# Causal attention on one Trainium2 core: heads normalised on GpSimd, stacked in pairs and projected together

## The chip, the cores and the metric

The kernel runs on 1 core of one Trainium2 chip. The metric is the device time of one execution in microseconds, the median of several runs.

## What is computed

`x` is 4 batches of 1024 tokens of 128 features, fp32. It is layer-normalised to `xn`, and the output is `x` plus two branches of `xn`. The branch that the change touches is causal attention with 16 heads of 64:

```python
normed = x / l2 * dim ** 0.5 * gamma
qkv = (normed @ w_qkv).reshape(b, n, 3, h, d)
sim = jnp.einsum('bhid,bhjd->bhij', q, k)      # q scaled by d ** -0.5
sim = jnp.where(causal_mask, mask_value, sim)
attn = jax.nn.softmax(sim, axis=-1)
out = jnp.einsum('bhij,bhjd->bhid', attn, v)
return out.reshape(b, n, h * d) @ w_out
```

The other branch is a mixture of 8 experts (two chosen per token, 128 to 512 to 128), added to `xn` and layer-normalised.

## The kernel before

It has four stages: `routing` (normalisation, the transposed normed tokens `nT` with an fp32r high and low part, the router, the slots for each expert), `attention([0], True, xn)` for the first pair of heads with fp32 probabilities ("native"), `experts`, and `attention([1..7], False, None)` for the other seven pairs with split probabilities. Each engine walks the same hand-written order (`beside`, L799) and takes from it what is its own; all waits are on semaphores.

**Units and chunks.** The work of attention is cut in units, one head of one batch: 8 in the first call, 56 in the second (G = 8 units per pair of heads, `g // 2` the batch, `g % 2` the head of the pair). A unit has 12 chunks of score work. For a chunk, PE multiplies keys and queries into one of two `score_ps` banks (L1298, L1299), ACT takes the exponent into `probs` and, in the second call, once more into `p_hi` (L1082, L1084), POOL masks a diagonal block (L1024) and subtracts `p_lo` (L1032), and four chunks later (LAG) PE multiplies with the values into `head_ps` (L1318 to L1327). Row 64 of the values is one, so row 64 of `head_ps` holds the sums, the softmax's denominators.

**Maxima.** Beside unit g, PE computes the scores of unit g + 1 a first time, tile by tile (8 tiles at the chunks of `MAX_AT`, L770, L1281), DVE takes their negated maxima (L1140), and SP moves each as a row into `q_b` (`shifts`, L927), where it enters the real scores as one more contraction row. A first tile's pass waits until DVE has taken the last of the unit before.

**Projections.** Even units hold the four q and k projections of the next batch (chunks 0, 1, 3, 5; `PROJECT_AT`, L773), odd units the two value projections (chunks 1 and 5; L1262, fp32, from `nT`). ACT takes high parts (L1057, L1061, L1066), DVE low parts (L1114, L1126), and SP copies q and k high parts to the second operands by DMA, 4 of 256 KB after the fourth projection (`copies`, L936, L937), all in SBUF.

**Output.** ACT copies `head_ps` (65 rows, values and sums) to `heads` (L1095). In the unit after, at chunks 7, 9 and 11 (`Y_AT`, L789), PE multiplies it with `wo` (65 rows, 129 columns: the weights of one head and a one in the corner, so that column 128 is the sum) in tiles of 128 tokens (L1341), DVE inverts column 128 (L1191) and adds rows times inverse to `acc` (L1199).

**Combine steps.** In the second call, groups of six units bring the experts' results in: POOL gathers rows (L1008) in the second and third unit, DVE centres rows of `x` in the third (L1156, chunks 2, 4, 5, 6), and the other steps lie in units 3, 5 and 7 from the group's start.

```python
            PROJECT_AT = [{0: 0, 1: 1, 3: 2, 5: 3}, {1: 4, 5: 5}]
...
            COMBINE_AT = [(2, c) for c in (2, 4, 5, 6)]
...
            Y_AT = [7, 9, 11]
            y_units = [(0, 3), (3, 3), (6, 2)]
```

## Time and profile before

| | us |
|---|---|
| median of 3 runs | 1457.95 (1456.97 to 1460.27) |
| the profiled execution | 1463.13 |
| its span, first to last instruction | 1461.4 |
| PE busy | 1351.4 (92%) |
| DVE busy | 1038.1 (71%) |
| ACT busy | 947.8 (65%) |
| POOL busy | 867.2 (59%) |
| first attention call, on PE | 66 to 242 |
| second attention call, on PE | 394 to 1457 |

Busy is the time in which an engine works on instructions; issuing DMAs, waiting and branching do not count. The profile also gives PE's granted clock as a share of 2.4 GHz, 0.958 over the whole span. In a timeline a row is one instruction or a few alike, with its start, its duration and, in brackets, the idle time ahead of it and what ended it. In a group, the number after the bar is the idle time ahead of its instructions. SPq is SP's DMA queue; its duration is that of the issue, not of the transfer.

### The profile page before, as it was taken

How to read it: one execution, taken by the hardware profiler on the slowest of the kernel's cores; microseconds unless marked ns; L12 is line 12 of the kernel's file. 1: busy time of each engine (PE TensorE's matmuls, PEld its weight loads, DVE VectorE, ACT ScalarE, POOL GpSimd, SP SyncE). 2: the span in 40 equal slices, each digit the busy share in tenths (PEclk: the TensorE clock that was granted, in tenths of full speed). 3: DMA queues.
4: the chain of work that ended last, by engine and by line, in shares of the span. 5: the costliest groups of instructions: out<-in, count | busy, mean ns of one | idle time of the engine just before them, and what ended most of it. 6: DMA issues, size and time to landing. Idle time of an engine off the chain costs nothing.

```text
span 1461.4 us, 27770 instructions
## 1 busy us (share of the span) xinstructions
PE 1351.4 (92%) x8360; PEld 1124.9 (77%) x8361; DVE 1038.1 (71%) x2674; ACT 947.8 (65%) x2094; POOL 867.2 (59%) x1304
## 2 busy tenths in 40 slices
PE   4569998999879999999999899899899999899998
PEld 4446666999757888788788788788788788788886
DVE  5656654222257788888888888888888888888773
ACT  2435544555447677677777677677677777677775
POOL 3426651332227568667667667767766766766666
PEclk9669999999869999999999999999999999999999
DMA  6222221222122022112112212112212212211112
GB/s 204 89 60 63 63 54 55 77 75 77 47 57 52 3 41 50 29 30 51 35 33 44 43 30 46 38 36 42 41 30 46 42 32 39 48 30 32 30 30 59
DMA packets 131078, 72.47 MB, mean 50 GB/s; under 512 B 80216, under 2 KB 116864, under 8 KB 130944
## 3 DMA queue, kind: packets, MB, share of 16 engines
q1 hardware_dynamic: 114304, 54.18, 18.2%
q0 software_dynamic: 4096, 8.40, 1.9%
q10 hardware_dynamic: 12544, 8.29, 1.9%
q8 instruction: 62, 1.02, 0.3%
q14 instruction: 72, 0.59, 0.1%
HBM read 20.47 MB, written 16.52 MB: 25 GB/s over the span
## 4 chain that ended last, share of the span: by engine, by line
PE 53%; DVE 11%; issue 5%; ACT 2%; DMA 1%; SPq 0%; DVEq 0%; POOLq 0%; ACTq 0%
PE max_ps L1281 8%; PE score_ps L1299 6%; PE score_ps L1298 6%; PE misc_ps L1341 6%; PE head_ps L1318 5%; PE head_ps L1327 5%; PE head_ps L1325 5%; PE head_ps L1323 5%; DVE max_ps L1140 4%; PE misc_ps L1262 3%; DVE x_row L1156 2%; PE misc_ps L1256 2%; DVE q_a L1126 1%; PE misc_ps L1257 1%; PE misc_ps L1258 1%
## 5 line engine op out<-in xcount | busy, mean ns | idle before, releaser
L1032 POOL TENSOR_TENSOR p_lo<-probs,p_hi 128x512 fp32r<-128x512 f32 (+3 forms) x560 | 536.1, 958 | 188.5 <-ACT p_hi L1084 183.9
L1082 ACT ACTIVATE probs<-score_ps 128x512 f32<-128x512 f32 (+3 forms) x768 | 377.5, 492 | 257.0 <-PE score_ps L1299 243.8
L1140 DVE CUSTOM_DVE_ANT_0 max_ps<-max_ps,mask 128x128 f32<-128x128 f32 (+7 forms) x512 | 390.7, 763 | 111.1 <-PE max_ps L1281 87.8
L1298 PE MATMUL score_ps<-q_a,k_a 128*128 128x512 f32 (+3 forms) x768 | 304.3, 396 | 0.2 <-ACT p_hi L1084 0.2
L1281 PE MATMUL max_ps<-k_a,q_a 128*128 128x512 f32 (+3 forms) x768 | 238.6, 366 | 54.2 <-DVE shift L1140 45.0
L1024 POOL TENSOR_SCALAR_AFFINE_SELECT probs<-probs 128x128 f32<-128x128 f32 x512 | 153.7, 300 | 202.3 <-ACT p_hi L1084 136.9
L1299 PE MATMUL score_ps<-q_b,k_b 65*128 65x512 f32 (+3 forms) x768 | 269.6, 351 | 0.0
L1084 ACT ACTIVATE p_hi<-score_ps 128x512 fp32r<-128x512 f32 (+3 forms) x560 | 263.1, 470 | 0.0
L1318 PE MATMUL head_ps<-probs,v_all 128*65 128x128 f32 (+3 forms) x1088 | 248.7, 310 | 0.0
L1281 PEld LDWEIGHTS max_ps<-k_a,q_a 128*128 128x128 f32 x768 | 140.8, 195 | 114.9 <-DVE shift L1140 86.5
L1323 PE MATMUL head_ps<-p_hi,v_hi 128*65 128x512 f32 (+3 forms) x560 | 210.3, 376 | 0.0
L1327 PE MATMUL head_ps<-p_lo,v_hi 128*65 128x512 f32 (+3 forms) x560 | 183.8, 328 | 0.0
L1325 PE MATMUL head_ps<-p_hi,v_lo 128*64 128x512 f32 (+3 forms) x560 | 183.3, 327 | 0.0
L1298 PEld LDWEIGHTS score_ps<-q_a,k_a 128*128 128x128 f32 x768 | 146.9, 191 | 45.7 <-issue 15.7
L1299 PEld LDWEIGHTS score_ps<-q_b,k_b 65*128 65x128 f32 x768 | 147.5, 192 | 23.7 <-issue 10.8
L1199 DVE SCALAR_TENSOR_TENSOR acc<-misc_ps,rden,acc 128x128 f32<-128x128 f32 x512 | 150.2, 346 | 6.8
L1318 PEld LDWEIGHTS head_ps<-probs,v_all 128*65 128x65 f32 x1088 | 136.8, 138 | 21.7 <-issue 1.5
L1341 PE MATMUL misc_ps<-wo,heads 65*128 65x129 f32 x1024 | 149.1, 280 | 2.6 <-ACT heads L1095 1.5
L1341 PEld LDWEIGHTS misc_ps<-wo,heads 65*128 65x128 f32 x1024 | 142.9, 196 | 9.6 <-issue 2.9
L1095 ACT ACTIVATE heads<-head_ps 65x512 f32<-65x512 f32 x128 | 76.1, 595 | 43.4 <-PE head_ps L1327 26.4
L530 POOL CAST w_now<-w1T 128x1024 fp32r x39 | 40.6, 1042 | 106.0 <-PE hidden L664 87.8
L1126 DVE TENSOR_TENSOR q_a<-misc_ps,q_a 64x512 fp32r<-64x512 f32 x128 | 88.3, 690 | 20.9 <-ACT q_a L1057 17.0
(165 smaller groups left out, 2086.6 us busy)
## 6 DMA issues: line engine op xcount, KB each, us to landing
k_a<-k_a SPq DMA_DIRECT2D x64, 256.0 KB
q_b<-q_a SPq DMA_DIRECT2D x64, 256.0 KB
q_b<-shift SPq DMA_DIRECT2D x512, 0.5 KB
sorted_x<-zeros SPq DMA_DIRECT2D x13, 384.0 KB, 5.0
rows<-sorted_x SPq DMA_DIRECT2D x39, 128.0 KB, 2.1
sorted_y<-result ACTq DMA_DIRECT2D x39, 128.0 KB, 1.8
acc<-in_L_attn_x_dram SPq DMA_DIRECT2D x4, 512.0 KB, 7.2
x_row<-in_L_attn_x_dram SPq DMA_DIRECT2D x8, 256.0 KB
```

The lines of the kernel that those rows point to most:

```text
L1032: pool.tensor_tensor(p_lo[:, lo_slot(g, c), w0:w1], probs[:, slot, w0:w1], p_hi[:, slot, w0:w1].bitcast(F32), ALU.subtract).then_inc(pool_ ...
L1082: ins = act.activation(probs[:, slot, 0:width], src[:, 0:width], ACT.Exp, scale=SCALE)
L1084: ins = act.activation(p_hi[:, slot, FROM[c]:width], src[:, FROM[c]:width], ACT.Exp, scale=SCALE)
L1140: dve.tensor_tensor_reduce(out=max_ps[:, at:at + width], in0=max_ps[:, at:at + width], in1=mask[:, SEQ - width:SEQ], scale=-1.0, scalar=-M ...
L1281: ins = pe.matmul(max_ps[:, at + k0:at + k1], q_a[i][s][:, t * P:(t + 1) * P], k_a[i][s][:, k0:k1], start=True, stop=True)
L1298: pe.matmul(dst, k_a[i][s][:, keys], q_a[i][s][:, qs], start=True, stop=False)
L1299: pe.matmul(dst, k_b[i][s][:, keys], q_b[i][s][:, qs], start=False, stop=True).then_inc(scores_ready, 1)
L1318: ins = pe.matmul(head_ps[0:HEAD + 1, q0:q0 + end], v_all[i][:, j, s], probs[:, slot, 0:end], start=(j == 0), stop=(c in LAST and not SPLI ...
L1323: pe.matmul(head_ps[0:HEAD + 1, cols], v_hi[i][:, j, s], p_hi[:, slot, w0:width], start=(j == 0 and not DIAG[c]), stop=False)
L1325: pe.matmul(head_ps[0:HEAD, cols], v_lo[i][:, j, s], p_hi[:, slot, w0:width], start=False, stop=False)
L1327: ins = pe.matmul(head_ps[0:HEAD + 1, cols], v_hi[i][:, j, s], p_lo[:, lo_slot(g, c), w0:width], start=False, stop=c in LAST)
L1341: ins = pe.matmul(dst[:, t * (D + 1):(t + 1) * (D + 1)], heads[:, g % 2, q0:q0 + P], wo[:, g % 2], start=True, stop=True)
```

## The change

**Heads of a pair together.** `heads` becomes `raw`, with the same ACT copy. For each unit W but the last two of each call (`stacks`):
- in unit W + 1, chunk 5, SP moves the sums, row 64 of `raw`, by DMA to `sums`, 128 partitions of 8; at chunk 8 DVE inverts them (`invert`); at chunk 10 SP writes them to `inverse_row` in DRAM;
- in unit W + 2, chunk 0, SP reads that row back into `rden_all`, once for each of 64 partitions; after chunks 3 and 4 POOL multiplies `raw` by it, 64x512 each, into rows 0 to 63 or 64 to 127 of `stacked` (`normalise`), and waits for each of the two to end;
- in the odd unit W + 2 of a pair's second head, at chunks 7 and 9, PE multiplies `stacked` (128 rows) with `wo` (both heads' weights, 128 columns), four tiles each, and DVE adds each bank to `acc` in one addition of 128x512 (`add_y`).

The last pair of each call goes the old way (`last_y`, with `wo_last`).

**Values' tokens.** `nT` is kept no longer. `routing` stores it in DRAM (`nT_dram`, 8 DMAs of SP), and ACT's queue loads 512 KB per batch into `tokens` in the even unit ahead of the value projections. The freed space holds `probs` and `rden_all`, so the first exponents and the first spread wait for the stores.

**Order.** One order runs over all pairs of a call. The q and k projections come half by half (q and k of tokens 0 to 511, then the others), and the copies are 4 of 128 KB after the second projection and 4 after the fourth. At the start of a call only tiles 0 to 3 of the first unit's maxima stand ahead of the first score; the other four come in its chunks 0 and 1, and the next unit's maxima at chunks 2 to 10. The last batch's output is stored in three pieces. Additions of `acc` by combine steps and by `add_y` wait for each other.

```diff
+            HALF_TILES = TILES // 2
+            FIRST_MAX_AT = [0, 0, 1, 1]
+            SECOND_MAX_AT = [2, 3, 4, 5, 6, 7, 8, 10]
-            Y_AT = [7, 9, 11]
+            Y_AT = {7: 0, 9: 1}
+            LAST_Y_AT = {8: 0, 10: 1, 11: 2}
+            def stacks(W):
+                return W0 <= W < WL - 2
+                    if W % 2 and c in Y_AT and stacks(W - 2):
+                        order += [(kind, W // 2 - 1, Y_AT[c]) for kind in ("y", "add")]
+                    if stacks(W - 1):
+                        order += [(kind, W - 1, 0) for kind, at in (("sums", 5), ("invert", 8), ("inverse", 10))
+                                  if at == c]
+                    if stacks(W - 2):
+                        order += [(kind, W - 2, n) for kind, n, at in (("spread", 0, 0), ("norm", 0, 3),
+                                                                      ("norm", 1, 4)) if at == c]
...
+                        if kind == "project" and c in (1, 3):
+                            copies(g, c // 2)
+                        if kind == "shift":
+                            shifts(g, c)
+                        if kind == "sums":
+                            W = g
+                            sp.wait_ge(heads_out[0], W + 2)
+                            sp.wait_ge(heads_out[1], W + 2)
+                            sp.dma_start(sums[:, W % 2], raw[HEAD:HEAD + 1, W % 2]).then_inc(sums_moved[W % 2], 16)
+                        if kind == "inverse":
+                            sp.wait_ge(sums_inverted, n_stacked(W) + 1)
+                            sp.dma_start(inverse_row[W % 2].rearrange("(p j) -> p j", p=P), inverse[:, W % 2]
+                                         ).then_inc(inverse_moved[W % 2], 16)
+                        if kind == "spread":
+                            sp.wait_ge(inverse_moved[W % 2], n_spread(W) * 16)
...
+                                sp.wait_ge(norm_done, 2 * n_stacked(W - 1) + 2)
+                            sp.dma_start(rden_all[:], inverse_row[W % 2].partition_broadcast(HEAD)
+                                         ).then_inc(spread[W % 2], 16)
...
+                    def normalise(W, half):
+                        s, cols = W % 2, slice(half * BANK, (half + 1) * BANK)
+                        rows = slice(s * HEAD, (s + 1) * HEAD)
+                        if half == 0:
+                            pool.wait_ge(spread[s], n_spread(W) * 16)
...
+                        pool.tensor_tensor(stacked[rows, cols], raw[0:HEAD, s, cols], rden_all[:, cols],
+                                          ALU.mult).then_inc(norm_done, 1)
+                        pool.wait_ge(norm_done, 2 * n_stacked(W) + half + 1)
...
+                    def load_tokens(Q):
...
+                        act.dma_start(tokens[:], nT_dram[:, cols]).then_inc(tokens_loaded, 16)
...
+                    def invert(W):
+                        dve.wait_ge(sums_moved[W % 2], n_spread(W) * 16)
+                        if W - W0 >= 2:
+                            dve.wait_ge(inverse_moved[W % 2], n_spread(W - 2) * 16)
+                        dve.reciprocal(inverse[:, W % 2], sums[:, W % 2]).then_inc(sums_inverted, 1)
+                    def add_y(Q, n):
...
+                        dve.tensor_tensor(rows, misc_ps[u % 2][:].rearrange("p (t d) -> p t d", d=D), rows,
+                                          ALU.add).then_inc(y_added, 1)
...
+                    def project_pair(Q, n):
...
+                            ins = pe.matmul(dst[:, q * D:(q + 1) * D], stacked[:, q0:q0 + P], wo[:],
+                                            start=True, stop=True)
```

**DVE, from the end of chunk 5 of an even unit.** Before: the last of the projections' low parts is ahead, `ISA max_ps,shift` are the maxima of tiles 5 to 7, and an additions' block follows each.

```order
L1140 ISA max_ps,shift<-max_ps,mask 128x768 [waits max_scores,max_taken]
L1140 ISA shift 128x1
L1191 RECIPROCAL rden<-misc_ps_2 128x3 [waits misc_ready]
L1199 SCALAR_TENSOR_TENSOR acc<-misc_ps_2,rden,acc 128x128 [waits recip_done]
L1199 SCALAR_TENSOR_TENSOR acc<-misc_ps_2,rden,acc 128x128 x2
```

Now:

```order
L1186 ISA max_ps,shift<-max_ps,mask 128x768 [waits max_scores,max_taken]
L1186 ISA shift 128x1
L1186 ISA max_ps,shift<-max_ps,mask 128x896 [waits max_scores,max_taken]
L1186 ISA shift 128x1
L1237 RECIPROCAL inverse<-sums 128x8 [waits inverse_moved1,sums_moved1]
L1186 ISA max_ps,shift<-max_ps,mask 128x1024 [waits max_scores,max_taken]
L1186 ISA shift 128x1
L1186 ISA max_ps,shift<-max_ps,mask 128x128 [waits max_scores,max_taken]
```

The additions are gone from the even unit, and the wait for the sums' DMA stands ahead of the last maximum.

**SP, the same two units.** `q_b_2<-shift` are the shifts, `k_a_2<-k_a_2` and `q_b_2<-q_a_2` the copies. Before:

```order
L936 DMA k_a_2<-k_a_2 64x1024 [waits hi_done]
L937 DMA q_b_2<-q_a_2 64x1024
L936 DMA k_a_2<-k_a_2 64x1024
L937 DMA q_b_2<-q_a_2 64x1024
L927 DMA q_b_2<-shift 1x128x1 [waits max_taken] x16
```

Now, from the second copies of an even unit to the spread of the next:

```order
L931 DMA k_a_2<-k_a_2 64x512 [waits hi_done]
L932 DMA q_b_2<-q_a_2 64x512
L931 DMA k_a_2<-k_a_2 64x512
L932 DMA q_b_2<-q_a_2 64x512
L923 DMA q_b_2<-shift 1x128x1 [waits max_taken]
L949 DMA sums<-raw 128x1x8 [waits heads_out1,heads_out0]
L923 DMA q_b_2<-shift 1x128x1 [waits max_taken] x2
L953 DMA inverse_row<-inverse 128x8 [waits sums_inverted]
L923 DMA q_b_2<-shift 1x128x1 [waits max_taken]
L963 DMA rden_all<-inverse_row 64x1024 [waits norm_done,inverse_moved1]
```

The sums' DMA stands behind the copies and a shift.

**POOL, chunks 2 to 5 of a unit without gathers.** Before, with the masks (`AFFINE_SELECT`) and the splits (`p_lo`):

```order
L1032 TENSOR_TENSOR p_lo<-probs,p_hi 128x256 [waits pv_done]
L1024 AFFINE_SELECT probs<-probs 128x128 [waits probs_ready]
L1032 TENSOR_TENSOR p_lo<-probs,p_hi 128x128 [waits pv_done]
L1032 TENSOR_TENSOR p_lo<-probs,p_hi 128x512 [waits pv_done,probs_ready]
L1024 AFFINE_SELECT probs<-probs 128x128 [waits probs_ready]
```

Now:

```order
L1070 TENSOR_TENSOR p_lo<-probs,p_hi 128x256 [waits pv_done]
L1061 AFFINE_SELECT probs<-probs 128x128 [waits probs_ready]
L1070 TENSOR_TENSOR p_lo<-probs,p_hi 128x128 [waits pv_done]
L1033 TENSOR_TENSOR stacked<-raw,rden_all 64x512 [waits pool_split,diag_masked,misc_ready,spread0]
L1070 TENSOR_TENSOR p_lo<-probs,p_hi 128x512 [waits pv_done,probs_ready,norm_done]
L1033 TENSOR_TENSOR stacked<-raw,rden_all 64x512 [waits diag_masked,pool_split]
L1061 AFFINE_SELECT probs<-probs 128x128 [waits norm_done,probs_ready]
```

A multiply stands behind each of the splits of chunks 3 and 4.

## Rows read from the trace of the kernel before

**Rows 1.** Busy time by stretch: us, busy per engine (x instructions), clock, DMA share
```profile
420.00:1449.00 1029.00, 994.26 (x6190) 829.84 (x6189) 842.59 (x2144) 755.33 (x1670) 707.49 (x1069) 0.98 0.20 38
...
1361.00:1398.00 37.00, 37.00 (x239) 31.58 (x238) 26.58 (x68) 29.14 (x65) 24.52 (x38) 1.00 0.18 30
...
1243.00:1261.00 18.00, 15.81 (x87) 12.72 (x86) 17.21 (x32) 11.67 (x26) 14.86 (x22) 0.91 0.38 78
```

**Rows 2.** Waits of PE, 420 to 1449 us: us in total, times, longest
```profile
PE max_ps L1281 <- DVE shift L1140: 33.5, 44, 2.2
```

**Rows 3.** Timeline of PE, one output projection: start us, us, engine, line
```profile
901.69 0.83 PE L1341 MATMUL misc_ps<-wo,heads 65*128 65x129 f32 x6
902.36 0.38 PE L1318 MATMUL head_ps<-probs,v_all 128*65 128x128 f32 x2
```

**Rows 4.** Timeline of PE, the maxima's first pass, in two successive units
```profile
1387.67 0.22 PE L1281 MATMUL max_ps<-k_a,q_a 128*128 128x128 f32 x1
...
1405.56 0.23 PE L1281 MATMUL max_ps<-k_a,q_a 128*128 128x128 f32 x1
```

**Rows 5.** Timeline of PE, the same pass, and a wait, around a unit that centres rows
```profile
906.04 0.23 PE L1281 MATMUL max_ps<-k_a,q_a 128*128 128x128 f32 x1
...
920.75 0.81 PE L1281 MATMUL max_ps<-k_a,q_a 128*128 128x512 f32 x2 [2.15 <-DVE shift L1140]
...
928.23 0.22 PE L1281 MATMUL max_ps<-k_a,q_a 128*128 128x128 f32 x1
```

**Rows 6.** Groups by line and shape: xcount, busy us, mean ns, idle before
```profile
L1032 POOL TENSOR_TENSOR p_lo<-probs,p_hi 128x512 fp32r<-128x512 f32 x224 | 288.4, 1287 | 185.9 <-ACT p_hi L1084 183.9 <-PE head_ps L1327 1.4
...
L1199 DVE SCALAR_TENSOR_TENSOR acc<-misc_ps,rden,acc 128x128 f32<-128x128 f32 x512 | 150.2, 346 | 6.8
...
L1114 DVE TENSOR_TENSOR v_lo<-misc_ps,v_hi 128x512 fp32r<-128x512 f32 x56 | 38.7, 692 | 67.7 <-ACT v_hi L1066 67.7
```

**Rows 7.** Timeline of POOL, chunks 3, 4 and 6 of an even unit
```profile
1210.94 0.47 POOL L1032 TENSOR_TENSOR p_lo<-probs,p_hi 128x128 fp32r<-128x128 f32 x1
...
1213.45 1.29 POOL L1032 TENSOR_TENSOR p_lo<-probs,p_hi 128x512 fp32r<-128x512 f32 x1 [2.04 <-ACT p_hi L1084]
...
1216.34 1.28 POOL L1032 TENSOR_TENSOR p_lo<-probs,p_hi 128x512 fp32r<-128x512 f32 x1 [1.35 <-ACT p_hi L1084]
```

**Rows 8.** Timeline of ACT, SP and DVE, chunks 5 to 10 of the unit of rows 4
```profile
1396.54 1.21 ACT L1057 ACTIVATE k_a<-misc_ps 64x512 fp32r<-64x512 f32 x2
...
1399.61 1.21 SPq L937 DMA_DIRECT2D q_b<-q_a  x1
...
1400.56 1.10 DVE L1140 CUSTOM_DVE_ANT_0 max_ps<-max_ps,mask 128x896 f32<-128x896 f32 x1
...
1403.44 1.23 DVE L1140 CUSTOM_DVE_ANT_0 max_ps<-max_ps,mask 128x1024 f32<-128x1024 f32 x1 [0.26 <-PE max_ps L1281]
```

**Rows 9.** DMA issues: xcount, KB each, median us from issue to landing
```profile
sorted_x<-zeros SPq DMA_DIRECT2D x13, 384.0 KB, 5.0
rows<-sorted_x SPq DMA_DIRECT2D x39, 128.0 KB, 2.1
```

**Rows 10.** Timeline of PE and DVE at the starts of both attention calls
```profile
80.95 0.79 PE L1281 MATMUL max_ps<-k_a,q_a 128*128 128x128 f32 x2 [3.74 <-DMA q_b<-q_a]
...
83.50 0.70 DVE L1140 CUSTOM_DVE_ANT_0 max_ps<-max_ps,mask 128x512 f32<-128x512 f32 x1
...
92.25 0.63 PE L1298 MATMUL score_ps<-q_a,k_a 128*128 128x512 f32 x1
...
408.66 0.79 PE L1281 MATMUL max_ps<-k_a,q_a 128*128 128x128 f32 x2 [3.79 <-DMA q_b<-q_a]
```

**Rows 11.** Timeline of DVE and POOL, unit of rows 5
```profile
914.92 1.78 DVE L1156 TENSOR_SCALAR x_row<-x_row,mean,rstd 128x128 f32<-128x128 f32 x1
...
915.31 1.30 POOL L1032 TENSOR_TENSOR p_lo<-probs,p_hi 128x512 fp32r<-128x512 f32 x1
```

**Rows 12.** Timeline of SP: the last store
```profile
1457.79 0.37 SPq L968 DMA_DIRECT2D out_dram<-acc  x1
```

More of the change, by code:

```diff
@@ L89, in attention_and_experts @@
         zeroed = sem("zeroed")
+        nT_stored = [sem(f"nT_stored{i}") for i in range(BATCH)]
+        tokens_loaded = sem("tokens_loaded")
         dve_step = sem("dve_step")
@@ new lines, in attention @@
+            order = ([(kind, Q0, n) for n in range(6) for kind in ("project", "project_lo")]
+                     + [("max", W0, t) for t in range(HALF_TILES)] + [("shift", W0, t) for t in range(HALF_TILES)])
+            for at in range(W0 * CH, WL * CH + LAG):
+                order += beside(at // CH, at % CH)
+            order += [(kind, WL - 1, n) for n in range(len(y_units)) for kind in ("last_y", "last_add")]
+            misc = [o for o in order if o[0] in ("project", "y", "last_y")]
@@ L1360, in _ @@
-                    run(walk, pe)
+                    for kind, g, c in order:
+                        if kind == "score":
+                            score(g, c)
+                        elif kind == "max":
+                            max_scores_of(g, c)
+                        elif kind == "project":
+                            project(g, c)
+                        elif kind == "pv":
+                            values(g, c)
+                        elif kind == "y":
+                            project_pair(g, c)
+                        elif kind == "last_y":
+                            project_last(g, c)
```

643 lines of the change are left out of this document (330 added, 313 removed).

## The prediction

> **What bounds the kernel now.** I read the busy time by stretch first. From 420 to 1449 us, nearly all of the second attention call with its 56 units, PE is busy for 994.26 of 1029 us at a granted clock of 0.98, and in a stretch without combine steps for 37.00 of 37.00 us, while DVE, ACT and POOL have 26.58, 29.14 and 24.52 us [rows 1]. So there each microsecond taken from PE comes off the time until another engine is in the way, and ACT (79%) is the next one. Second, PE's waits: in that call it waits for hardly anything but DVE's maxima, 33.5 us in 44 waits [rows 2]. Third, the lengths of units: an undisturbed even unit takes 1405.56 - 1387.67 = 17.89 us [rows 4]; one in which DVE also centres rows takes 928.23 - 906.04 = 22.19 us, though PE waits only 2.15 us in it [rows 5]. The other 2 us or so go with PE at 1.2 in place of 2.4 GHz for a while after such a wait: the granted clock is 0.91 in a stretch around another such unit, where it is 1.00 in the stretch without [rows 1]. A wait of 2 us therefore costs 4.3 us. That price matters below.
>
> **Term A, the output projection.** Six PE records of one projection go by in 902.36 - 901.69 = 0.67 us, 0.112 us each [rows 3] (the modelled durations overlap; the step is what counts). Before, 64 units issue 16 records each, 1024. Now 30 pairs issue 16 each, and the last pair of each call, 4 units, still 16 each: 544. 480 records fewer, of 0.112 us: **-53.8 us**, 48.4 of it in the second call. The 128 rows in place of 65 lengthen no stream, since the step follows the columns (128 for 129). All of it lies on the path by rows 1, since PE has no idle time there to swallow it. It comes out of even units alone: they lose all 16 records, odd ones keep their number.
>
> **Term B, the starts of the calls.** PE now waits 3.74 and 3.79 us for the last copy before the first maximum [rows 10]. The copies of the first half now start two projections earlier and land while PE still projects the values, so these waits go. The first score comes 92.25 - 80.95 = 11.3 us after the first maximum [rows 10]; now it needs only tiles 0 to 3, taken by 83.50 + 0.70 = 84.2, and their shifts' landing, some 2.1 us like the shortest in rows 9: 86.3, up to 5.9 us earlier. But the four maxima put off run in unit 0 on a DVE that has 12 of them there, so I let most of that be given back. 5 us per call, **-10 us**; bounds 0 and -2 x (3.75 + 5.9) = -19.
>
> **Term C, the end.** The last store is 512 KB, issued at 1457.79 [rows 12] in a span of 1461.4: 3.6 us. Its last piece is now 128 KB, which takes 2.1 us from issue to landing [rows 9]. **-1 us**.
>
> **Term D, DVE's relief.** A unit's 8 additions of about 0.29 us (150.2 us over 512) [rows 6] and three reciprocals become, per pair, two additions of 128x512 from PSUM, like the 692 ns of v_lo [rows 6], and two small reciprocals. DVE loses some 2 us per unit. Of the 33.5 us of waits, 6 x 2.15 lie in the units with centring, ahead of the place where the additions stood; about 17 us are small waits of 0.2 to 1.2 us in other units, and half of them should go: **-8 us** (0 to -20).
>
> **Term E, the new wait on DVE.** This is the term that I trust least. `invert` stands in DVE's order at chunk 8, ahead of the last maximum, and waits for the denominators' DMA. SP issues that DMA at chunk 5, in even units behind the four copies of the second half and one shift. In the unit of rows 4, ACT ends the last key copy at 1396.54 + 1.21 = 1397.75, and the fourth 256 KB copy has been issued at 1399.61 + 1.21 = 1400.8 [rows 8]; with copies of half the size the fourth may be through in half that time, 1400.2. The shift's issue adds about the 0.37 us of another short issue [rows 12], and landing at least 2.1 us [rows 9]: 1402.7 to 1403.3, and up to 0.6 us later if the sums queue behind what the copies still move. `invert` takes 0.2, and the maximum of 1024 columns, which can start only then, 1.23 [rows 8]: it ends at 1404.1 to 1405.3, with its read of 0.1 at 1404.2 to 1405.5. PE needs it at the next unit's first maximum, which now comes 1.78 us earlier, at 1405.56 - 1.78 = 1403.8 [rows 4]. PE waits 0.4 to 1.7 us; I take 0.9, in 27 even units of the second call: **+24 us** (11 to 46). In odd units SP has no copies ahead of the sums, and the same chain ends before chunk 8. The rest of the relay (inverse sums to DRAM at chunk 10, spread at chunk 0, 256 KB) has until chunk 3's multiply; it fits with about 1 us over, and POOL's gap there takes as much again.
>
> No row shows in what order two DMAs of one queue move. The Trainium skill, DMA: Bandwidth & Descriptors, "Two DMAs through the same engine are not ordered", says that the descriptors of one queue of one DMA engine start in order; by that the sums' would start behind the copies', at the late end of this range, and the whole sum would be 22 us higher (46 for 24).
>
> **Term F, POOL.** 120 multiplies of 64x512 are new. No row shows one; between 128x128 at 0.47 us [rows 7] and 128x512 at 1287 ns [rows 6] I take 1.29, since a lane does its 512 columns. 2.6 us per unit, on an engine with 24.52 us of 37 [rows 1]. They stand behind the splits of chunks 3 and 4: in the unit shown POOL is idle 2.04 us ahead of chunk 4's split and 1.35 us ahead of chunk 6's [rows 7], and PE reads a split only four chunks after its score. So they are **free** there. Without that cover they would cost up to 2.6 us a unit. In the 16 units with gathers the gaps are filled; I add **+3 us** (0 to 20).
>
> **Term G, ACT.** 29.14 us of 37 over an even and an odd unit [rows 1] leave room, but an even unit shrinks to about 16.1 us with ACT's projection copies and one token DMA more in it, and PE has only two score banks. 0.1 us per even unit: **+3 us** (0 to 14). The token loads (512 KB per pair of units) and the store of nT lie beside other work: DMA is busy 20% [rows 1].
>
> **Sum**: -53.8 - 10 - 1 - 8 + 24 + 3 + 3 = -42.8. The profiled execution took 1463.1 us (span 1461.4), so 1420.3 for it. The median of the runs is 1457.95, 5.2 below; the forecast for the runs is **1415 us**. Its own range, from the bounds that can go together, is 1400 to 1435.
>
> **The rivals.**
> 1. *The sums land in time* (chance 0.27). If small DMAs overtake the tail of the copies or land in under 1.5 us, Term E is gone: 1391. For it: no row shows so small a DMA, and 2.1 us is what 128 KB take. Against it: the fourth copy's issue ends 3 us after ACT's last key copy [rows 8], however soon the sums land.
> 2. *Slower: DVE waits over 2 us in every even unit* (0.10). The same place, another price. At the 5.0 us that rows 9 show for 384 KB, the sums land at about 1406, PE waits 3 us, and like the unit of rows 5 the clock falls after it; at the 4.3 us of such a unit or more, 27 x 4.3 = 116 in place of 24: 1507. It decides from 24 + 43 = 67 us, 2.5 us per even unit, so from a wait of some 2 us with its loss of clock. Against it: 4 KB are not 384.
> 3. *The multiplies hold DVE* (0.10). In the units with centring, a DVE operation of 128x128 between SBUF tiles takes 1.78 us while POOL's 1.30 us split runs beside it, and ends as that ends [rows 11]. If three of the four centrings of each of the 8 units meet one multiply more, 3 x 1.29 x 8 = 31: 1446. For it: POOL is without gaps there. Against: POOL waits for its own multiply, which leaves a gap for DVE. The Trainium skill, GPSIMD Engine Reference, "Key points", says that GpSimd shares its SBUF interfaces with VectorE, with contention for DVE instructions in a two-port mode or with two SBUF inputs; the row agrees with it.
> 4. *POOL is late* (0.05): the spread lands after POOL has reached the multiply, and PE waits for splits, 1 us in half the units: 1443.
>
> **How the numbers follow.** The forecast has 0.48. 1380 to 1455 holds it, rivals 1, 3 and 4 with their spread, and leaves out rival 2 and the far ends, together under 0.2. A measurement of this kernel tells 0.2%, 2.9 us, from no change. Slower is rival 2 and a tail of 3 and 4: 0.12. Within 0.2%: 0.03. Faster: 0.85. That the change does not do what it says has one place only, the last pair of each call, and it is in Term A.
>
> **What would show it.** Right: 544 records of the projection; PE's busy time in the second call 45 to 50 us lower; even units some 16.8 to 17 us, odd ones near 17; a DVE wait of `inverse` for the sums' DMA, in even units alone, followed by a PE wait at the next unit's first maximum. Rival 1: no such wait, even units near 16.2. Rival 2: those waits near 3 us and the clock below 0.95 in the second call. Rival 3: centring operations over 2 us. Rival 4: POOL's `stacked` waiting for the spread. Wrong altogether: PE's busy time unchanged, or ACT as the one that PE waits for.

## The result: 1559.5 us, slower by 100 us, and the profile after

The changed kernel takes 1559.53 us (median of 4 runs, 1557.23 to 1563.08) where the kernel before took 1459.11 on the same chip: a ratio of 1.069, 95% interval 1.066 to 1.072. The forecast was 1415. The profiled execution of the change took 1560.88 us.

The page of the change: busy time, the clock row and the DMA line.

```profile
PE 1365.7 (88%) x7880; PEld 1108.6 (71%) x7881; DVE 944.4 (61%) x2134; ACT 940.2 (60%) x2094; POOL 1015.3 (65%) x1424
...
PEclk9679999999688998999999999899899999899999
...
DMA packets 169509, 107.67 MB, mean 69 GB/s; under 512 B 101240, under 2 KB 138144, under 8 KB 169376
```

PE issues 7880 matmul records where it issued 8360: the 480 records are gone. But its clock row falls to 8 in the second call, where before it stands at 9, and POOL has 1015 us where it had 867. The busy time by stretch of the second call (columns as in [rows 1]), and its waits:

```profile
420.00:1549.00 1129.00, 1013.31 (x5767) 817.49 (x5765) 762.51 (x1662) 748.02 (x1670) 840.42 (x1177) 0.94 0.26 60
```

```profile
PE max_ps L1345 <- DVE shift L1186: 100.4, 75, 3.3
DVE inverse L1237 <- DMA sums<-raw: 72.5, 26, 3.4
...
DVE x_row L1206 <- DMA two_y<-sorted_y,slots: 29.4, 8, 4.0
...
ACT raw L1143 <- POOL stacked L1033: 22.0, 10, 3.2
...
PE score_ps L1362 <- DMA q_b<-shift: 5.0, 1, 5.0
```

The stretch takes 1129 us where the 1029 us of [rows 1] did the same work. PE waits 100.4 us for maxima in place of 33.5 [rows 2]. Two waits on DVE are new: for the sums (72.5 us) and for the gathered rows (29.4 us in 8 waits of up to 4.0). One on ACT is new as well: its copy of `head_ps` into `raw` waits for the POOL multiply that still reads that buffer (22.0 us in 10). One place at a time.

**The end of an even unit.** Timeline of SP's queue, from the copies of the second half on:

```profile
1494.85 0.50 SPq L931 DMA_DIRECT2D k_a<-k_a  x1
...
1496.68 0.60 SPq L932 DMA_DIRECT2D q_b<-q_a  x1
1497.32 0.62 SPq L923 DMA_DIRECT2D q_b<-shift  x1
1498.04 0.57 SPq L949 DMA_DIRECT2D sums<-raw  x1
```

DVE, in the same stretch:

```profile
1501.86 0.20 DVE L1237 RECIPROCAL inverse<-sums 128x8 f32<-128x8 f32 x1 [3.07 <-DMA sums<-raw]
1502.05 1.23 DVE L1186 CUSTOM_DVE_ANT_0 max_ps<-max_ps,mask 128x1024 f32<-128x1024 f32 x1
```

PE, in the same stretch:

```profile
1503.49 0.30 PE L1345 MATMUL max_ps<-k_a,q_a 128*128 128x128 f32 x1 [1.79 <-DVE shift L1186]
```

Four copies and a shift are issued ahead of the sums, which go out at 1498.04 and release the reciprocal 3.8 us later. The maximum of 1024 columns stands behind it, and PE waits 1.79 us. Two units earlier the same wait also costs clock. Timeline of PE, the first pass of the maxima at three successive units:

```profile
1447.39 0.23 PE L1345 MATMUL max_ps<-k_a,q_a 128*128 128x128 f32 x1
...
1466.00 0.30 PE L1345 MATMUL max_ps<-k_a,q_a 128*128 128x128 f32 x1 [1.68 <-DVE shift L1186]
...
1484.74 0.22 PE L1345 MATMUL max_ps<-k_a,q_a 128*128 128x128 f32 x1
```

Busy time in the stretch behind the wait (the third last number is the clock):

```profile
1466.00:1470.50 4.50, 4.50 (x24) 4.17 (x25) 1.54 (x5) 1.46 (x4) 1.33 (x3) 0.68 0.28 59
```

The even unit takes 18.61 us where [rows 4] show 17.89. The odd one behind it takes 18.74 us without a further wait, because PE runs at a mean of 0.68 of 2.4 GHz for 4.5 us, so partly at 1.2 GHz. PE waits like this at the start of 20 of the odd units, mostly for 1.7 to 2.0 us.

**Unit 3 of each group of six**, the one with the first steps behind the centring. Timeline of POOL, the second multiply of the unit ahead and the last gather:

```profile
845.10 1.25 POOL L1033 TENSOR_TENSOR stacked<-raw,rden_all 64x512 f32<-64x512 f32 x1
...
853.81 0.97 POOL L1044 DMA_INDIRECT two_y<-sorted_y,slots  x1 [0.16 <-issue]
```

DVE, the first combine steps:

```profile
857.02 2.88 DVE L1206 SCALAR_TENSOR_TENSOR x_row<-two_y,weights,x_row 128x128 f32<-128x128 f32 x2 [3.65 <-DMA two_y<-sorted_y,slots]
```

PE, and below it the busy time of the unit:

```profile
860.36 0.80 PE L1345 MATMUL max_ps<-k_a,q_a 128*128 128x512 f32 x1 [3.27 <-DVE shift L1186]
```

```profile
852.60:877.80 25.20, 20.69 (x115) 16.59 (x114) 16.48 (x34) 12.63 (x30) 17.27 (x26) 0.86 0.10 22
```

The unit begins at 852.6; POOL issues the last gather 1.2 us into it. In the kernel before that came at 925.59, 2.6 us ahead of the unit that starts at 928.23 [rows 5]. DVE waits 3.65 us for it ahead of a maximum, PE 3.27 us, and the clock is 0.86 over a unit of 25.2 us. Before, the unit took 18.9.

The lengths of all units, from first pass to first pass, show where the 100 us lie. Means over seven groups, in us, units 0 to 5 of a group: 18.2, 17.6, 21.4, 19.1, 17.9 and 17.4 before; 18.9, 20.3, 20.6, 25.2, 19.0 and 18.8 in the change. Units 1 and 3 lose most, unit 2 even gains.

**The start of the second call**, in PE's timeline:

```profile
415.32 0.76 PE L1362 MATMUL score_ps<-q_a,k_a 128*128 128x512 f32 x1 [3.09 <-DMA q_b<-shift]
...
434.16 0.77 PE L1362 MATMUL score_ps<-q_a,k_a 128*128 128x512 f32 x1 [5.03 <-DMA q_b<-shift]
```

The waits of [rows 10] for the copies are gone, but the score of chunk 4 waits 5.03 us for the shifts of the unit's own tiles.

### The profile page after: what moved, and what is told of

The parts are those of the page before. It is cut to its first block, busy times and chain, and to the rows that moved or that the text cites. A ratio compares the mean times of both kernels' runs of the same rounds, so it can differ in the third digit from the quotient of the medians.

```text
span 1559.2 us, 27266 instructions
## 1 busy us (share of the span) xinstructions
PE 1365.7 (88%) x7880; PEld 1108.6 (71%) x7881; DVE 944.4 (61%) x2134; ACT 940.2 (60%) x2094; POOL 1015.3 (65%) x1424
## 3 DMA queue, kind: packets, MB, share of 16 engines
q1 hardware_dynamic: 148128, 72.65, 19.8%
## 4 chain that ended last, share of the span: by engine, by line
PE 37%; DVE 12%; issue 8%; DMA 6%; POOL 4%; SPq 4%; ACT 3%; DVEq 0%; POOLq 0%; ACTq 0%
PE max_ps L1345 6%; DMA sums<-raw 4%; DVE max_ps L1186 4%; PE score_ps L1363 4%; PE score_ps L1362 4%; PE head_ps L1392 4%; PE head_ps L1390 4%; PE head_ps L1388 3%; PE misc_ps L1326 3%; PE head_ps L1383 3%; PE misc_ps L1403 2%; DVE x_row L1206 2%; POOL p_lo L1070 2%; PE misc_ps L1318 2%; DMA two_y<-sorted_y,slots 2%
## 5 line engine op out<-in xcount | busy, mean ns | idle before, releaser
L1345 PE MATMUL max_ps<-k_a,q_a 128*128 128x512 f32 (+3 forms) x768 | 247.8, 379 | 114.3 <-DVE shift L1186 113.8
L1362 PE MATMUL score_ps<-q_a,k_a 128*128 128x512 f32 (+3 forms) x768 | 314.1, 409 | 20.9 <-DMA q_b<-shift 15.8
L1363 PE MATMUL score_ps<-q_b,k_b 65*128 65x512 f32 (+3 forms) x768 | 275.3, 358 | 0.0
L1383 PE MATMUL head_ps<-probs,v_all 128*65 128x128 f32 (+3 forms) x1088 | 256.8, 319 | 0.5 <-POOL probs L1061 0.5
L1388 PE MATMUL head_ps<-p_hi,v_hi 128*65 128x512 f32 (+3 forms) x560 | 217.6, 389 | 1.7 <-POOL p_lo L1070 1.6
L1383 PEld LDWEIGHTS head_ps<-probs,v_all 128*65 128x65 f32 x1088 | 144.4, 143 | 33.3 <-issue 1.9
L1033 POOL TENSOR_TENSOR stacked<-raw,rden_all 64x512 f32<-64x512 f32 x120 | 153.5, 1279 | 15.8 <-POOL p_lo L1070 6.5
L1143 ACT ACTIVATE raw<-head_ps 65x512 f32<-65x512 f32 x128 | 76.2, 596 | 102.3 <-PE head_ps L1392 66.8
L1172 DVE TENSOR_TENSOR q_a<-misc_ps,q_a 64x512 fp32r<-64x512 f32 x128 | 88.2, 689 | 36.9 <-ACT q_a L1094 34.2
L1172 DVE TENSOR_TENSOR k_b<-misc_ps,k_a 64x512 fp32r<-64x512 f32 x128 | 87.8, 686 | 19.8 <-ACT k_a L1094 18.8
L1392 PEld LDWEIGHTS head_ps<-p_lo,v_hi 128*65 128x65 f32 x560 | 78.9, 141 | 28.3 <-issue 3.0
```

The source lines that it names most:

```text
L1172: ins = dve.tensor_tensor(lo, src[s * HEAD:(s + 1) * HEAD, :], hi, ALU.subtract)
L1345: ins = pe.matmul(max_ps[:, at + k0:at + k1], q_a[i][s][:, t * P:(t + 1) * P], k_a[i][s][:, k0:k1], start=True, stop=True)
L1362: pe.matmul(dst, k_a[i][s][:, keys], q_a[i][s][:, qs], start=True, stop=False)
L1363: pe.matmul(dst, k_b[i][s][:, keys], q_b[i][s][:, qs], start=False, stop=True).then_inc(scores_ready, 1)
L1383: ins = pe.matmul(head_ps[0:HEAD + 1, q0:q0 + end], v_all[i][:, j, s], probs[:, slot, 0:end], start=(j == 0), stop=(c in LAST and not SPLI ...
L1388: pe.matmul(head_ps[0:HEAD + 1, cols], v_hi[i][:, j, s], p_hi[:, slot, w0:width], start=(j == 0 and not DIAG[c]), stop=False)
```

## The experiments

The theory at the outset: three places where something small stands behind something large in an engine's order. The rival: POOL's multiplies hold the units themselves. All kernels of this part ran beside the kernel before, and each time is a median. Some build on others; each says on which. Units of a group are counted from its start, unit 0: the "third" (unit 3) holds the first steps behind the centring, the "second" (unit 2) the last gathers and the centring, and the "first" (unit 1) the last 13 steps of the group before.

**The sums, three ways**, on the change as it was.

```diff
-  (("sums", 5), ("invert", 8), ("inverse", 10))
+  (("sums", 5), ("invert", 10), ("inverse", 10))   # first
+  (("sums", 4), ("invert", 8), ("inverse", 10))    # second
+  (("sums", 4), ("invert", 10), ("inverse", 10))   # third
```

> The edit: DVE inverts the sums at chunk 10, behind the unit's last maximum, in place of chunk 8, ahead of it; nothing else moves. Theory A (the reciprocal that waits for the sums' DMA holds back the last maximum, and PE with it, and the clock falls after that wait): PE's waits at the next unit's first maximum go from 1.8 to under 0.5 us in the 27 even units of the second call, and 1.5 us of half-speed clock go with each: 27 x 3.3 = 89 us less than the change's 1560, so about 1470. Theory B (POOL, with 2.6 us of multiplies more per unit, is what holds the even units): the reciprocal's place is of no matter, the time stays within 10 us of 1560. Theory C (the stall moves: the wait for the inversion now stands in SP's order ahead of the last shift and the spread, which come later): the DVE wait goes, another takes half of it back, about 1515.

> The edit: SP issues the sums' DMA at chunk 4, ahead of the four copies of chunk 5, in place of behind them; the inversion stays at chunk 8. Theory A (the sums come late because they stand behind the copies on SP's queue): DVE's wait for the sums in even units goes (28 waits, 80 us before), the landing is 2 us as in odd units in place of 3.8, and the time is about 1470 as with the late inversion. Theory B (POOL): within 10 us of 1560. Theory D (the landing of 4 KB is late for another reason, the spread or the tokens' load on the same engines): the wait stays at over 2 us and the time within 20 us of 1560.

> Both edits: the sums' DMA at chunk 4, the inversion at chunk 10. Theory A: the two take away one and the same wait, so the time is within 10 us of the better of the two single ones, about 1465. If they add up (say 1510 each alone and 1465 together), each hides a part of its own. Theory B: about 1560.

Measured: 1501.3, 1497.0 and 1498.6 us (ratios to the kernel before 1.028, 1.025, 1.026, each with 0.003 either way). Each of the two edits alone takes off some 60 us, both together no more: one wait, as Theory A had it, though 60 us and not 89. Theory A counted 3.3 us for each of 27 even units with the odd one behind it. By the means of the second kernel, units 0 and 1 together get 3.0 us shorter and units 4 and 5 together 3.4, but units 2 and 3 only 0.4: there unit 3 waits for the gathered rows all the same, and keeps its 25.2 us. Theory B falls for the units without that second stall. Of Theory C something is left: in the first kernel POOL waits for the spread, 14.1 us in 8 waits in the second call. The same place in the second kernel, on SP's queue:

```profile
1426.97 0.54 SPq L949 DMA_DIRECT2D sums<-raw  x1
1428.01 0.51 SPq L931 DMA_DIRECT2D k_a<-k_a  x1
```

DVE in the same unit:

```profile
1431.81 0.20 DVE L1237 RECIPROCAL inverse<-sums 128x8 f32<-128x8 f32 x1
```

PE, the first pass of the maxima around the odd unit ahead of it:

```profile
1400.87 0.23 PE L1345 MATMUL max_ps<-k_a,q_a 128*128 128x128 f32 x1
...
1417.90 0.22 PE L1345 MATMUL max_ps<-k_a,q_a 128*128 128x128 f32 x1
```

The sums go out ahead of the copies, and the reciprocal waits for nothing. The odd unit takes 17.03 us, where it took 18.74.

**The sums on ACT's queue.** Base: the change. The DMA is ACT's in place of SP's, at chunk 5, then at 6, then at 7.

```diff
-  sp.dma_start(sums[:, W % 2], raw[HEAD:HEAD + 1, W % 2])
+  act.dma_start(sums[:, W % 2], raw[HEAD:HEAD + 1, W % 2])
```

> The change as it was, but the sums' DMA is issued on ACT's queue at chunk 5, behind ACT's copies of the fourth projection, in place of SP's queue at the same chunk behind the four copies of k and q; the inversion stays at chunk 8. Theory Q (what makes the sums late in even units is their place on SP's queue: four issues of 0.6 us and a shift ahead of them, and 512 KB of copies on the same queue): DVE's waits for the sums, 80 us in 28, fall under 20 us, and the time is within 15 us of the kernel with the DMA at chunk 4, about 1500. Rival (the DMA engines are busy with the copies, whichever queue the sums are on): the waits stay over 50 us and the time over 1535.

> As the kernel with the sums on ACT's queue (1497 us), but one chunk later, at chunk 6, so that they are issued while SP issues the copies. Order of one queue: on a queue of their own the sums land 1.9 to 2.2 us after their issue in even units too, DVE waits for them little or not, time 1495 to 1505. Load of the DMA engines: they land 3 us or more after their issue, as on SP's queue behind the copies, DVE waits for them in most even units, 10 us in all or more.

> As the last kernel, with the sums' DMA at chunk 7 of ACT's order, so that it is issued about 1.5 us after the first copy, ahead of the tokens' load on its own queue. Order of one queue: it lands 2 us or so after its issue, the reciprocal waits under 0.5 us or not at all, time about 1497. Load of the DMA engines: it lands 3 us or more after its issue, DVE waits 1 us or more for it in even units (20 us or more in all), time 1505 or more.

Measured: 1496.9, 1496.6 and 1499.0 us; DVE waits for the sums in no unit of the three. In the first two ACT's queue issued them 1.2 and 0.5 us ahead of SP's first copy, so these tell the place only. In the third they go out in the middle of the copies. ACT's queue:

```profile
1435.43 0.48 ACTq L1135 DMA_DIRECT2D sums<-raw  x1
```

SP's queue, the first and the last copy:

```profile
1434.76 0.50 SPq L931 DMA_DIRECT2D k_a<-k_a  x1
...
1436.58 0.60 SPq L932 DMA_DIRECT2D q_b<-q_a  x1
```

DVE:

```profile
1438.55 0.20 DVE L1236 RECIPROCAL inverse<-sums 128x8 f32<-128x8 f32 x1
```

The trace has the landing of these issues: this one lands 2.4 us after it went out, where on SP's queue behind the copies it was 3.8 us to the reciprocal. Over the 27 even units of the second call the median is 2.4 us, over the odd ones, without copies, 1.9. So beside copies in flight on another queue the sums lose 0.5 us, behind them on the same queue some 1.8. That speaks for the order of the queue and against the load of the DMA engines, with two limits: here only two copies had been issued ahead of the sums, not four, and in six second units, beside POOL's gathers, they took 2.8 to 4.9 us on ACT's queue as well.

**The first combine steps three chunks later**, on top of both edits of the sums:

```diff
-  COMBINE_AT += [(g, c) for g in (3, 5) for c in (0, 0, 1, 2, 3, 4, 5, 5, 6, 7, 8, 9, 11, 11)]
+  COMBINE_AT += [(3, c) for c in (3, 3, 4, 4, 5, 5, 6, 7, 8, 9, 10, 10, 11, 11)]
+  COMBINE_AT += [(5, c) for c in (0, 0, 1, 2, 3, 4, 5, 5, 6, 7, 8, 9, 11, 11)]
```

> Both edits as before, and in the third unit of each group of six the combine steps that read the gathered rows begin at chunk 3 in place of chunk 0 (the last two of the fourteen end at chunk 11 as before). Theory A2 (a second stall: POOL's multiplies make the gathers 3 us late, DVE waits 3.7 us for them ahead of a maximum, PE waits 3.3 us and the clock falls): those 9 units go from 25.2 us to about 19, so 8 x 6 = 48 us less than the kernel with both edits, about 1420. Theory B2 (POOL is short of time in these units whatever DVE does): PE then waits for the splits in place, and not more than 15 us come back.

Measured: 1459.4 us, ratio 0.9998 (0.9983 to 1.0012), so 39 us less. The third units go from 25.2 us and more to between 19.8 and 21.0, by Theory A2. These two repairs bring the kernel to the time of the one before, and no lower.

**The own shifts ahead of the copies**, on top of that:

```diff
   order += [("max", *item) for item in max_items(W, c)]
+  order += [("shift", *item) for item in max_items(W, c) if item[0] == W]
...
-  order += [("shift", *item) for item in max_items(W, c - 1)]
+  order += [("shift", *item) for item in max_items(W, c - 1) if item[0] > W]
```

> On top of the same kernel: in the first unit of each call SP issues the shifts of that unit's own tiles 4 to 7 right behind their maxima, ahead of the four copies of the next batch's first half, in place of behind them. Theory S (the start's gain is given back because those shifts stand behind the copies on SP's queue, and the score of chunk 4 waits 5.05 us for them in the second call): that wait falls under 2 us, 3 to 5 us less per call, 6 to 10 in all, about 1451. Rival (the maxima themselves are late, DVE at 2.17 us waits there): the wait keeps its place, under 2 us of gain.

Measured: 1442.4 us, ratio 0.989 (0.987 to 0.991), 17 us less where 6 to 10 were expected; the profiled executions differ by 11 (1453.5 and 1442.8). SP's queue at the start of the second call, without the edit (copies, then the shifts):

```profile
419.04 0.50 SPq L932 DMA_DIRECT2D k_a<-k_a  x1
...
421.53 2.54 SPq L924 DMA_DIRECT2D q_b<-shift  x4
```

With it:

```profile
409.57 3.26 SPq L925 DMA_DIRECT2D q_b<-shift  x2
413.37 0.50 SPq L933 DMA_DIRECT2D k_a<-k_a  x1
```

The last own shifts now stand ahead of the copies, and the wait of 5 us for them is gone.

**The multiplies on DVE**, at chunks 4 and 5, on top of the kernel with the late first steps, then with the own shifts too, then on the change as it was:

```diff
-  if o[0] == "norm": normalise(o[1], o[2])       # in POOL's walk
+  elif kind == "norm": normalise(g, c)           # in DVE's walk, dve.tensor_tensor
-  ("norm", 0, 3), ("norm", 1, 4)
+  ("norm", 0, 4), ("norm", 1, 5)
```

> On top of the last kernel (sums' DMA at chunk 4, inversion at chunk 10, first combine steps at chunk 3): DVE does the multiplies into stacked, at chunks 4 and 5, in place of POOL at 3 and 4. Theory L (POOL's longer work stretches the combine steps: DVE operations of 128x128 between SBUF tiles take 0.8 to 1.2 us while POOL works on its tiles, 172 us of DVE in all in place of 137 before the change): those rows go back to about 137 us or below, the units with combine steps get 2 us shorter on average over 16 to 24 of them, time about 1425. Rival (DVE becomes the bound: 120 multiplies of some 0.7 us or, if they are stretched beside POOL's splits, 1.3 us are added to an engine that has 17 of 19.2 us in the first unit of each group): those units grow by 1.4 to 2.6 us each, time 1475 or more.

> Both of the two edits above. If they are independent, their gains add: about 1417 by theories L and S. If DVE is the bound at the start as well, the sum falls short by what the multiplies put ahead of the maxima of the first units.

> The change as it was, with nothing moved but the multiplies into stacked, which DVE does at chunks 4 and 5. Theory A2 (POOL's multiplies are what delays the gathers by 3 us, so that DVE waits for them in the third unit of each group): DVE's 8 waits for two_y, 29 us in the change, fall under 5 us in all and those units go from 25.2 to about 20; the waits for the sums in even units stay (80 us or somewhat less). Time about 1560 - 40 = 1520. Rival (the gathers are late because their data lands late, behind the 35 MB of new transfers): the waits for two_y stay near 29 us, the time near 1560.

Measured: 1546.0, 1531.3 and 1538.9 us. Theory L's remedy fails and its rival holds: 87 and 89 us slower than the same kernels with POOL. The group of the multiplies on DVE, in the first of the three:

```profile
L1245 DVE TENSOR_TENSOR stacked<-raw,rden_all 64x512 f32<-64x512 f32 x120 | 136.9, 1145 | 12.1 <-DMA rden_all<-inverse_row 10.4
```

137 us of DVE, 1145 ns each, where one that begins while POOL is idle takes 0.69 us (the row at 1423.69 of that trace). They stand ahead of maxima, and PE's waits for these are 115.8 us in the second call, in place of 48.3. In the third of the three, the waits for the gathered rows fall from 29.4 to 3.7 us, as Theory A2 had it, yet only 21 us come off. So the price of the multiplies was still open. The second of the three is 15 us faster than the first: the own shifts give the same again.

**The multiplies left out.** `stacked` holds ones; the relay and all waits stay. On top of the kernel of 1442 us, and on the change as it was:

```diff
-  pool.tensor_tensor(stacked[rows, cols], raw[0:HEAD, s, cols], rden_all[:, cols], ALU.mult).then_inc(norm_done, 1)
+  pool.sem_inc(norm_done, 1)
```

> On top of the kernel of 1442 us (sums at 4, inversion at 10, first steps at 3, own shifts first): POOL's 120 multiplies into stacked are left out (stacked holds ones; the relay of sums, inversion, spread and all waits stay). It prices the multiplies. Theory L (POOL's 2.6 us more per unit holds the units with gathers and stretches the combine steps): the three long units of each group (19.3, 20.0 and 20.6 us) fall together by 4 us or more, 8 x 4 = 32 us or more, so 1410 or less; units without combine steps stay at 16.8 and 17.05. Rival (those units are bound by DVE's own work and by gathers, as before the change, where they took 17.6, 22.2 and 18.9): less than 10 us come off, over 1432.

> The change as it was, with POOL's 120 multiplies left out (stacked holds ones; every wait stays). Theory M (the multiplies make the gathers late): DVE's waits for two_y, 29 us in 8, go to under 3 us, the third unit of each group from 25.2 to about 19.5; the waits for the sums stay, since they come from SP's queue. Time: 1559 - 8 x 5.5 (third units) - 36 (what the multiplies cost the repaired kernel, less some 10 us that are the same thing) = about 1490. Rival (the gathers are late for the DMA traffic): the third units keep 24 us or more, the time over 1530.

Measured: 1406.4 us (36 less) and 1507.4 us (52 less). Busy time of units 1, 2 and 3 of a group, in the kernel of 1442 us:

```profile
1091.30:1110.50 19.20, 17.68 (x115) 14.39 (x114) 16.99 (x35) 12.49 (x30) 15.31 (x22) 1.00 0.18 43
1110.50:1130.30 19.80, 17.35 (x95) 13.11 (x94) 14.97 (x30) 15.00 (x33) 17.25 (x23) 1.00 0.45 112
1130.30:1151.00 20.70, 17.98 (x116) 14.48 (x115) 16.77 (x33) 12.27 (x29) 18.38 (x26) 1.00 0.11 21
```

And without the multiplies:

```profile
1176.40:1193.90 17.50, 17.06 (x115) 14.51 (x114) 13.74 (x34) 12.02 (x29) 12.39 (x20) 1.00 0.15 35
1193.90:1211.60 17.70, 16.70 (x96) 13.21 (x94) 13.52 (x29) 14.73 (x33) 15.18 (x21) 1.00 0.56 129
1211.60:1230.50 18.90, 17.67 (x116) 14.54 (x114) 15.36 (x33) 12.45 (x30) 15.21 (x24) 1.00 0.14 30
```

In the first unit of the group, 1.7 us go; DVE, which does the same operations, is busy 3.3 us less in it. The 36 us are a low price: in two of the eight groups the second unit takes 23.8 and 23.4 us without the multiplies, where most others take 17.7; PE waits 3.0 us there for a maximum behind centrings, and its clock is 0.86. These 12 us are a new stall; without it, by this estimate, 48 would have come off. In the change as it was, the waits for gathered rows fall from 29.4 to 10.9 us, not to under 3, and the third units go from 25.2 to between 19.4 and 22.5 us, 4.6 on average, some 36 of the 52 us. Most of the rest is in the first units, 20.3 to 18.4 us on average. Theory M is right in kind and short in size; what else makes the gathers late, no run isolates. The waits for the sums stay (84.3 us).

**Where the steps stand.** On the kernel of 1442 us, gathers earlier; steps spread; both; and the kernel before with the same spread:

```diff
-  GATHER_AT = [(1, 8)] + [(1, c) for c in (9, 10, 11)] + [(2, c) for c in (1, 3, 5, 7, 9)]
+  GATHER_AT = [(1, 8)] + [(1, c) for c in (9, 10, 11)] + [(2, c) for c in (0, 1, 2, 5, 7)]
...
+  COMBINE_AT += [(3, c) for c in (3, 4, 5, 6, 7, 8, 9, 10, 11)]      # in place of the steps behind the centring
+  COMBINE_AT += [(4, c) for c in (7, 7, 8, 9, 9, 11)]
+  COMBINE_AT += [(5, c) for c in range(12)]
+  COMBINE_AT += [(6, c) for c in (7, 7, 9, 9, 10, 11)]
+  COMBINE_AT += [(7, c) for c in range(8)]
```

> On top of the same kernel of 1442 us: POOL issues the second unit's five gathers at chunks 0, 1, 2, 5 and 7 in place of 1, 3, 5, 7 and 9. Theory: POOL is behind from chunk 5 on in these units, because its multiplies stand there too; with two gathers less behind them, the last splits come earlier, 0.5 to 1 us less in each of 8 units, about 1437. Rival (POOL has the same work in all, and its early part delays the splits that PE waits for): 1442 or up to 8 us more.

> On top of the same kernel of 1442 us: the 41 combine steps behind the centring are spread over five units (9, 6, 12, 6 and 8) in place of three (14, 14, 13). DVE no longer has eight additions in even units, where it is now busy 12 of 16.8 us. Theory: the first unit of each group, which holds the last 13 steps and takes 19.25 us with DVE busy for 17, gets 1 to 2 us shorter, the third the same, and the two even units that take steps stay within 0.3 us: 8 x 2.5 = 20 us less, about 1422. Rival (each step is stretched wherever POOL works beside it, and the even units give it back): 1435 to 1450.

> The kernel of 1424.7 us with the second unit's gathers at chunks 0, 1, 2, 5 and 7. Alone this gave 2 us, within its uncertainty. Expected: 1420 to 1426. If the third unit, whose steps now begin thinner, no longer gains from it, 1425 or above.

> The kernel before, with nothing but the table of the combine steps as in the kernel of 1424.7 us (9, 6, 12, 6 and 8 steps in five units, the first behind chunk 3). Theory P (in the kernel before, even units hold eight additions with scaling on DVE, so they have no room for six steps more; and its gathers were in time): the time stays within 6 us of 1459, and the whole 34 us of the repaired kernel are owed to the pairing. Rival (the spread helps any kernel, since odd units lose two to five steps): 1445 or less, and the pairing is worth only the rest.

Measured: gathers early 1440.5 us, 2 less, inside the uncertainty. Spread: 1424.7 us, ratio 0.976 (0.974 to 0.979), 17.7 less, as expected. Both: 1427.4, nothing gained. The kernel before with the spread: 1441.2 us, ratio 0.989 (0.986 to 0.991). That went against Theory P: the spread helps the kernel before by 18 us as well. So of the 34 us between the best version, 1424.7, and the kernel before, 18 are the spread's, and the pairing with its three repairs is worth 16.5.

## Why the prediction was wrong, step by step

**What bounds the kernel** was right as to PE, and that it waits for DVE's maxima: in the best version still 27.8 us. ACT, named as the next engine in the way by its busy share, was not that: PE waits 5.0 us for it in the second call of the change, and 100.4 for the maxima.

**Term A** holds in its count (480 records) and its reach. Without stalls an odd unit takes 17.03 us, as forecast, and an even one 16.8. That this is also the 16.8 to 17 us of the forecast is luck: those were 16.1 with a wait of 0.9 on top. An even unit loses 1.1 us against [rows 4], not 1.79. The remaining 0.7 us are steps between matmuls beyond the shortest of their shapes: summed over an even unit, 2.5 us in the kernel of 1442 us, 1.7 in the one before. One, of 0.33 us, carries a wait for ACT's exponent; the others have no releaser in the trace. So **Term G** (0.1 us) was mis-sized at this place by 0.7, some 19 us over 27 units, as far as they are ACT's.

**Term B** (-10) failed on its second half. The waits for copies went, as said. But I looked for what gives the gain back on DVE, and it was on SP: the copies of the next batch stand ahead of the shifts of the unit's own second half. From the first projection to the start of its second unit, the second call took 439.49 - 393.58 = 45.9 us before and 448.95 - 397.90 = 51.1 in the change, so +5 in place of -5; with the shifts ahead it is 43.5. The first call, up to its third unit, took 65.2 and 65.5 us.

**Term C** (-1) is too small to be told apart: the last three stores are issued from 1555.12 on, and the span ends at 1559.2. **Term D** (-8) did not show: DVE's busy time in the second call fell from 842.6 to 762.5 us, but PE's waits for maxima are 43.4 us even in the kernel of 1442 us, against 33.5 [rows 2]. With the multiplies left out of that kernel they are 26.8: the relief was there, and the longer combine steps (below) took it.

**Term E** (+24, bounds 11 to 46) had the right place, the right order of events and the wrong price: 60 us. From the end of ACT's last key copy, 1494.82, to the reciprocal it is 7.0 us, where I had 5.0 to 6.2. The sums go out 3.2 us after that copy, and land 3.8 us later, not 2.1 to 2.7. PE's wait, mostly 1.7 to 2.0 us, lay at the edge of my range; that it also lowers the clock I had kept for waits of over 2 us, in rival 2. This is the step that failed in the term: it priced the wait alone, and the wait with its loss of clock costs some 3.2 us where nothing else holds the pair of units, nothing much where the rows are late too, and 60 / 27 = 2.2 us on average. The Trainium skill, DMA: Bandwidth & Descriptors, "Two DMAs through the same engine are not ordered", has descriptors of one queue start in order; the 3.8 us behind copies, and 2.4 us on another queue beside them, agree with it, and the price by it (46) was the nearer one.

**Term F** (+3, bounds 0 to 20) is the step that failed most. One multiply takes what I had estimated:

```profile
L1033 POOL TENSOR_TENSOR stacked<-raw,rden_all 64x512 f32<-64x512 f32 x120 | 153.5, 1279 | 15.8 <-POOL p_lo L1070 6.5 <-POOL probs L1061 1.0
```

But they are not free. Left out, they give back 52 us in the change and 36 in the repaired kernel. I had read POOL's gaps in a unit without combine steps [rows 7], and there the multiplies do fit. The 3 us for units with gathers rested on no row. There the multiplies push the last gather 3.9 us back against the unit's start (from 2.6 ahead of it to 1.2 behind). And, the mechanism of rival 3, they meet more of DVE's operations between SBUF tiles. The group that changed most, before and in the change:

```profile
L1184 DVE TENSOR_TENSOR acc<-acc,x_row 128x128 f32<-128x128 f32 x32 | 9.4, 292 | 1.1
```

```profile
L1230 DVE TENSOR_TENSOR acc<-acc,x_row 128x128 f32<-128x128 f32 x32 | 25.1, 784 | 3.5
```

292 ns became 784; with the multiplies left out it is 293 again. All eight groups of the combine steps on `x_row` and `acc` together took 146 us of DVE before, 172 in the change and 139 in the change without multiplies: 33 us more with the multiplies than without, near the 31 of rival 3. Rival 3 named the centrings for it, and these got shorter (1225 to 848 ns, 705 without multiplies); others paid. Such a lengthening costs only where a maximum stands behind it: in the best version the same groups take 182 us. The Trainium skill, GPSIMD Engine Reference, "Key points", which says that GpSimd shares SBUF interfaces with VectorE, agrees with the second row.

A third way was in no theory of mine, and no run takes it away alone: ACT's copy into `raw` waits for the multiply, 22.0 us in 10 waits in the change and 34.2 us in 17 in the kernel of 1442 us, all but two in second and third units, and none with the multiplies left out. PE's own waits for ACT or for POOL's splits stay at 0.8 us or less in the second and third unit looked at, and the first units, without any such wait, get 1.7 us shorter too when the multiplies go. So it is not the whole price; how the rest divides among late gathers, longer DVE operations and this wait stays open.

**The account.** Forecast -43. The sums cost 60, not 24 (+36). The multiplies cost 52, not 3 (+49). Term B was 0 and +5 in place of -10 (+15), Term G with its part of A +16, Term D +8. That would make +81 where +100 came out; the parts overlap, and 19 us are not assigned. Put the other way: the kernel with all three stalls mended and the multiplies left out takes 52 us less than the kernel before, of the 73 that Terms A to D promised. The gain was there, and was more than given back. Rival 2, at a tenth, had the direction and the place, and the second call's clock is below 0.95 as it said; but with 60 for its term the sum would still have been 1451, so it alone does not make the result. Rival 1 fell: in 26 of the 27 even units of the second call DVE waits for the sums. So did rival 4: in the change POOL's multiplies don't wait for the spread.

## What to carry to other kernels

When work is taken off the busiest engine and given to a chain of small DMAs and to idle engines, read each queue that the chain passes as one would read an engine: what stands ahead of a 4 KB transfer, and what stands behind the instruction that waits for it. Price an engine's new work in its fullest units, not in a typical one, and price what it does to its neighbour. The three stalls here were mended by moving a few entries of the order, and the best version, at 1424.7 us, beats both kernels.

## What the runs showed of the hardware that I had not expected

A PE wait of 1.7 us, shorter than the 2.15 us that I had read, was already followed by a clock of 0.68 over 4.5 us, but not each time: behind the wait of 1.79 us at 1503.49 the clock was 1.00 over as long a stretch. A 64x512 multiply on DVE takes 0.69 us begun while POOL is idle and up to 2.17 in the same kernel, longer than on POOL (1.28). A DMA on ACT's queue can overtake ACT's own work: in the first kernel with the sums on that queue, both copies of `k_a` stand ahead of them in ACT's order, in its timeline:

```profile
1430.49 0.59 ACT L1088 ACTIVATE k_a<-misc_ps 64x512 fp32r<-64x512 f32 x1 [0.16 <-PE misc_ps L1319]
1430.56 0.48 ACTq L1135 DMA_DIRECT2D sums<-raw  x1
1431.11 0.59 ACT L1088 ACTIVATE k_a<-misc_ps 64x512 fp32r<-64x512 f32 x1
```

The issue went out 0.55 us ahead of the start of the second copy.
